# Edge logits and their per-node maxima: the leaky slope outside the loop, two of ten chunks raised on VectorE

## What is computed

```python
xj = h[src]                                   # h = x @ Wn.T + bn
a = leaky_relu(sum((xj + ee) * attn, -1), 0.01)   # one logit per edge
m = segment_max(a, dst)                       # greatest logit of each destination node
a = exp(a - m[dst])                           # the next phase takes it from here
```

## Time and profile before

| | us |
|---|---|
| median of 3 runs (lowest, highest) | 4043.22 (4040.58, 4044.01) |
| the profiled execution | 4043.18 |
| its span, first to last instruction | 4041.4 |
| loop of `phase_logits`, first ACT instruction to the last L1281's end | 2016.9 to 2446.9 |
| from there to the start of L1299's copy and its end | 2469.3 and 2472.7 |

### The profile page before, as it was taken

The page is one execution under the profiler, slowest core; times in us unless marked ns, Lnnn a source line. Parts: engine busy times, 40 slices in busy tenths (PEclk is TensorE's granted clock), DMA queues, the critical chain, the costliest instruction groups (busy, mean ns, idle before and its releaser), DMA issues. The chain is left out here.

```text
span 4041.4 us, 85100 instructions
## 1 busy us (share of the span) xinstructions
PE 3184.0 (79%) x17887; PEld 2358.5 (58%) x17888; DVE 2484.0 (61%) x6663; ACT 1822.0 (45%) x6302; POOL 1312.2 (32%) x1050
## 2 busy tenths in 40 slices
PE   5666667899887767999843335889999899999978
PEld 4444446888776655767632224778888444444455
DVE  7999998888775553244488886777666400001754
ACT  1888882344455532011298874777776000000111
POOL 1788888888888700101000000000000100003922
PEclk9999999999998878999855557999999999999989
DMA  2444443667888854757565553544332543541057
GB/s 95 126 122 124 120 118 86 197 203 241 242 248 277 279 219 132 212 169 210 163 213 185 180 165 107 157 125 121 111 97 78 186 140 117 190 154 42 0 191 262
DMA packets 430402, 646.79 MB, mean 160 GB/s; under 512 B 102666, under 2 KB 286737, under 8 KB 430176
## 3 DMA queue, kind: packets, MB, share of 16 engines
q1 hardware_dynamic: 344348, 511.68, 41.0%
q10 hardware_dynamic: 54388, 122.22, 8.4%
q0 software_dynamic: 31568, 11.67, 3.3%
HBM read 436.88 MB, written 207.57 MB: 159 GB/s over the span
## 5 line engine op out<-in xcount | busy, mean ns | idle before, releaser
L1065 POOL DMA_INDIRECT slots<-all_B,put_index x800 | 1050.4, 1313 | 343.1 <-issue 338.9
L2340 PE MATMUL gio_po<-gio_T,all_A 125*128 125x500 f32 (+1 forms) x1400 | 531.0, 540 | 7.7 <-DMA gio_T<-pair 7.7
L2340 PEld LDWEIGHTS gio_po<-gio_T,all_A 125*128 125x128 f32 x1400 | 249.8, 190 | 285.7 <-issue 276.4
L1315 ACT ACTIVATE lm_raised<-lm_hot,srt_words 128x125 f32<-128x125 bf16 x1200 | 356.3, 385 | 83.7 <-DVE lm_top L1230 66.8
L1349 PE MATMUL lm_ps<-lm_v,lm_node 125*128 x1220 | 170.5, 184 | 267.2 <-DVEq L1217 95.0
L1036 PE MATMUL put_ps<-put_right_in,put_left_in 128*128 128x125 f32 x2210 | 320.1, 295 | 66.5 <-ACT put_left_in L893 65.8
L2073 PE MATMUL att_ps<-att_right,att_left 128*125 128x125 f32 x2380 | 313.6, 284 | 71.4 <-ACT att_right L2094 57.9
L2073 PEld LDWEIGHTS att_ps<-att_right,att_left 128*125 128x125 f32 x2380 | 283.4, 190 | 97.6 <-issue 86.8
L1036 PEld LDWEIGHTS put_ps<-put_right_in,put_left_in 128*128 128x128 f32 x2210 | 282.0, 202 | 90.8 <-ACT put_left_in L893 76.6
L2147 DVE SCALAR_TENSOR_TENSOR att_power<-soft_negated,srt_words,att_far 128x125 f32 (+1 forms) x1190 | 321.1, 345 | 3.8 <-ACT att_right L2094 3.3
L1651 PE MATMUL c_po<-c_halves,c_T 125*125 125x512 f32 x1250 | 320.1, 405 | 0.0
(11 more groups left out here) (454 smaller groups left out, 5596.5 us busy)
## 6 DMA issues: line engine op xcount, KB each, us to landing
c_T<-counts SPq DMA_DIRECT2D x255, 312.5 KB, 3.3
pair<-put_T ACTq DMA_DIRECT2D x125, 625.0 KB
att_ring<-hot SPq DMA_DIRECT2D x480, 160.0 KB
gio_T<-pair SPq DMA_DIRECT2D x60, 1250.0 KB, 5.8
hot<-put_hot SPq DMA_DIRECT2D x448, 160.0 KB
all_A<-in_edge_attr_dram SPq DMA_DIRECT2D x100, 448.0 KB
lm_planes<-src_rows SPq DMA_DIRECT2D x123, 320.0 KB, 3.6
counts<-put_T ACTq DMA_DIRECT2D x125, 312.5 KB
```

The lines of the kernel that those rows point to most:

```text
L1065: nc.gpsimd.indirect_dma_start(slots, bass.IndirectOffsetOnAxis(index[:, C * g + j:C * g + j + 1], 0), stage[:, C * g + j, :], None).then_ ...
L1315: ins = nc.scalar.activation(raised[:, j % 2, c * P:(c + 1) * P], hot[:, j, c * S:c * S + P], ACT.Copy, scale=logit[:, ds(G * g + c, 1)])
L2340: ins = t_.matmul(po[:, i % 2, h, 0:w], A[:, b, 128 * h:128 * h + 128], tiles, start=(b == 0), stop=(b == NB - 1))
```

## The change

The loop's two slope instructions go: `total` now ends with one instruction that subtracts `floor` from the sum, adds the edge's own term and writes the logit. `logit` then holds unsloped values over the floor (of unsloped sums). After the loop `slope` adds the floor back and applies the slope to the whole `logit` in place, and the same to the maxima of 125 x 25.

ACT raises eight chunks of ten (LIFTS = 8). DVE takes the running maximum of those with 128x1000 elements, and for the last two chunks multiplies one-hot by logit and takes the maximum in one instruction each, straight from `hot`. As DVE now reads `hot`, SP waits, before it loads into a ring slot, on `grouped` as well as on `lifted`; the head of `grouped` is 3 instead of 2, so that SP's `wait_ge(grouped, g + 1)` asks for DVE's `greater` of group g-3.

```diff
                         sp.wait_ge(lifted, g + 1)
+                        sp.wait_ge(grouped, g + 1)
                         sp.sem_inc(passed, 1)
...
-                    chain(v.tensor_tensor(z[:, :], z[:, :], logit[:, ds(G * g, G)], ALU.add))
-
-                def logits(chain, g):
                     at = logit[:, ds(G * g, G)]
-                    chain(v.scalar_tensor_tensor(z[:, :], z[:, :], 0.01, z[:, :], ALU.mult, ALU.max))
-                    v.tensor_scalar(at, z[:, :], floor[:, :], None, ALU.subtract).then_inc(ready, 1)
+                    v.scalar_tensor_tensor(at, z[:, :], floor[:, :], at, ALU.subtract, ALU.add).then_inc(ready, 1)
+
+                def slope(t, parts):
+                    chain(v.tensor_scalar(t, t, floor[0:parts, :], None, ALU.add))
+                    chain(v.scalar_tensor_tensor(t, t, 0.01, t, ALU.mult, ALU.max))
...
-                    dve.wait_ge(grouped, g + 2)
+                    dve.wait_ge(grouped, g + 3)
+                    w = LIFTS * P
                     if first:
-                        ins = v.tensor_copy(top8[:, :], lift)
+                        v.tensor_copy(top8[:, 0:w], lift[:, 0:w])
                     else:
-                        ins = v.tensor_tensor(top8[:, :], top8[:, :], lift, ALU.max)
+                        v.tensor_tensor(top8[:, 0:w], top8[:, 0:w], lift[:, 0:w], ALU.max)
+                    for c in range(LIFTS, G):
+                        chunk, top = hot[:, ds(g % RING, 1), c * S:c * S + P].rearrange("p a n -> p (a n)"), top8[:, c * P:(c + 1) * P]
+                        if first:
+                            ins = v.tensor_scalar(top, chunk, logit[:, ds(G * g + c, 1)], None, ALU.mult)
+                        else:
+                            ins = v.scalar_tensor_tensor(top, chunk, logit[:, ds(G * g + c, 1)], top, ALU.mult, ALU.max)
                     ins.then_inc(grouped, 1)
...
+                turns = turns_of(dve, k)
+                dve.wait_ge(lifted, turns * RING + 3)
+                chain = Chain(dve, sloped)
+                slope(logit, L)
                 dve.wait_ge(turned, 1)
                 v.tensor_reduce(greatest[:, :], ps[0:P, 0:NB * L].rearrange("p (b l) -> p b l", l=L), AX.X, ALU.max).then_inc(ended, 1)
                 dve.wait_ge(ended, 1)
+                slope(greatest[:, :], P)
...
-                        act.wait_ge(grouped, g + 1)
-                        for c in range(G):
+                        act.wait_ge(grouped, g + 2)
+                        for c in range(LIFTS):
```

More of the change, by code:

```diff
@@ L1144, in phase_logits @@
         bounded, gathered, floored, cleared = (s.sem(n) for n in ("bounded", "gathered", "floored", "cleared"))
-        split, chain_sem = s.sem("split"), s.sem("chain")
+        split, chain_sem, sloped = s.sem("split"), s.sem("chain"), s.sem("sloped")
         expanded, looked, summed, ready, lifted, grouped = (
@@ L1148, in phase_logits @@
         joined, passed, turned, ended = (s.sem(n) for n in ("joined", "passed", "turned", "ended"))
-        PZ = 4
+        PZ, LIFTS = 4, G - 2
         with nc.Block() as block:
@@ L1246, in _ @@
                 chain(v.tensor_reduce(low[:, 0:2], bank(7)[0:1, 0:2 * L].rearrange("p (t l) -> p t l", t=2), AX.X, ALU.min))
-                chain(v.tensor_tensor(low[:, 2:3], low[:, 0:1], low[:, 1:2], ALU.add))
-                v.scalar_tensor_tensor(low[:, 3:4], low[:, 2:3], 0.01, low[:, 2:3], ALU.mult, ALU.max).then_inc(bounded, 1)
+                v.tensor_tensor(low[:, 2:3], low[:, 0:1], low[:, 1:2], ALU.add).then_inc(bounded, 1)
                 dve.wait_ge(gathered, 2)
                 chain(v.tensor_copy(floor[:, :], bank(7)[:, 256:257]))
-                for sem, head in ((summed, PZ), (grouped, 2), (joined, 1), (expanded, 2)):
+                for sem, head in ((summed, PZ), (grouped, 3), (joined, 1), (expanded, 2)):
                     dve.sem_inc(sem, head)
@@ L1256, in _ @@
                 expand(2)
-                logits(chain, 0)
                 dve.wait_ge(ready, 1)
                 total(chain, 1)
-                logits(chain, 1)
                 n = chain.n
@@ L1264, in step @@
                 def step(g, first):
-                    chain = Chain(dve, chain_sem, n + 3 * g)
+                    chain = Chain(dve, chain_sem, n + g)
                     expand(g + 3)
@@ L1268, in step @@
                     total(chain, g + 2)
-                    logits(chain, g + 2)
                     greater(g, first)
-                    assert chain.n == 3
+                    assert chain.n == 1
                 with dve.Fori(0, NB) as d:
@@ L1279, in _ @@
                         step(g, False)
-                    dve.wait_ge(grouped, g1 + 2)
+                    dve.wait_ge(grouped, g1 + 3)
                     v.tensor_reduce(tops[:, ds(d, 1), :].rearrange("p a n -> p (a n)"),
@@ L1335, in _ @@
                 pe.wait_ge(bounded, 2)
-                t_.matmul(bank(7)[:, 256:257], ones[0:1, :], low[:, 3:4], start=True, stop=True).then_inc(gathered, 1)
+                t_.matmul(bank(7)[:, 256:257], ones[0:1, :], low[:, 2:3], start=True, stop=True).then_inc(gathered, 1)
                 pe.wait_ge(split, 1)
```

## The result

| | before | after |
|---|---|---|
| median of 9 runs each (lowest, highest), us | 4043.15 (4040.22, 4046.09) | 4051.22 (4047.16, 4057.93) |
| the profiled execution's span | 4041.4 | 4049.2 |
| loop: start of the copy to `floor` to the last block reduction's end | 441.2 | 440.8 |
| tail: from there to the start of the copy of the spread maxima | 22.5 | 27.1 |
| next phase (`att_...`): from the clearing of `all_total` to the start of DVE's last `all_B<-att_ps` copy | 643.0 | 649.6 |

A forecast was written before the change was run, and what follows sets the result against it. DVE was taken to set the loop's time at 2.94 us a step. To 4043.18 us came -1 ahead of the loop, +5 in it and +5.5 behind it, +9.5 in all: 4052.7 us, range 4040 to 4066.

The forecast's parts named there:

- DVE's step by itself: DVE's loop step without the added wait falls from 2.94 to 2.79 us, in 94 steps 14 us.
- The first step: A block's first loop step gains nothing: the 2.95 us to the next L1216 is PE's look-up time and stays.
- The wait: SP's added wait for the end of DVE's step: 3.04 us a step where it lasts, loop 3.6 us slower.
- the recurrence: Loop rule: a step starts at least 3.2 us (mean) after the end of the step two before; loop 3.6 us slower.
- Rival 3: SP's path is a tenth longer or a chunk instruction costs 0.30: loop +15 instead of +5, 4063 us; chance 0.15.
- The last steps: Loop steps at a block's end, where DVE reduces and SP catches up: 0.15 us less each, 3.6 us.
- Landings: In the loop, the one-hots' and planes' landings that hold SP now lie on the path: +1.4 us.
- the 1 ahead of it: Ahead of the loop, two slope pairs go: 1 us less.
- The tail: After the loop, the slope over all logits, partly covered by DVE's 5.70 us wait for PE, and over the maxima: +5.5 us.
- Rival 2: After the loop, writing every second word is slow: slope passes up to 18.6 us, tail +15, 4062 us; chance 0.13.
- The next phase: The attended phase behind the tail, with unchanged code: the sum had no term for it.

The follow-up runs named there:

- without SP's wait: The changed kernel without SP's added wait, DVE's two chunk instructions reading chunks that ACT raised instead of the one-hots: 4036.28 us, ratio 0.9986 to before.
- SP reordered: The changed kernel, all waits kept, with SP issuing the planes' part two indices ahead of the one-hots' part: 4036.57 us, ratio 0.9983 to before.
- The wait alone: The kernel before with only SP's added wait on DVE's maximum (`grouped`, head 3): 4052.80 us, ratio 1.0025.
- the kernel with 56 more instructions: The changed kernel with 56 unneeded semaphore increments in DVE's idle time ahead of the wait on `turned`: 4041.84 us, ratio 0.9995 to before.

## Why the prediction came out as it did

- **DVE's step by itself**: right. 2.84 in after and 2.83 without SP's wait, against 2.79, and 1.64 from the maximum to L1211 as was forecast; a chunk pair with the step back to L1211 takes 0.52 to 0.60, where 2 x 0.26 was summed.
- **The first step**: right for after. "It gains nothing" holds up to the next L1216: 2076.61 to 2079.64 in after is 3.03 us, and the step's own 0.18 us more is given back by a wait for PE that is gone. It hides only so much: with the slope in the loop as well, the same two chunks cost 0.55, and the stretch is 3.32 us.
- **The wait**: right in place and in kind, as waits of 18.2 us for SP and the reordering show. In the first and middle steps after lost 0.18 x 25 + 0.03 x 69 = 6.7 us against before; the recurrence, taken without the last steps, had about 7. Rival 3, the same recurrence with a longer path, is refuted by that. But the agreement is partly luck: DVE's own gain in these steps was 7 us (before against SP reordered), where 69 at 0.15 are 10, and the wait cost 14, where the recurrence had 17 to 18. The wait alone shows the same: 8.9 us where it gave 14.
- **The last steps**: mis-sized. They were summed at 0.15 less each, 3.6 us. They are 0.26 less, 6.3 us, because the idle time between the block reduction and the next expansion fell as well, to 0.61 us from 0.77.
- **Landings**, +1.4: on the path, and of that size, at one place. In SP's waits the one-hots' landing makes up 2.6 us in four waits.

```profile
SPq L1193 <- DMA lm_hot<-hot: 2.6, 4, 1.4
```

The longest, 1.4 us, ends at 2123.97, and DVE's expansion at 2125.12 then waits 1.39 us for SP, with no back edge in between. It is among the 6.7 us above. With all this the loop is -0.4 instead of +4 (the 5, less the 1 ahead of it): 2.7 of the difference are the last steps, and 1.9 the recurrence and the landings together.
- **The tail**: right, +4.7 against +5.5. It begins 1.17 us after the reduction (1.3 summed), the passes take 2.82 and 5.36 (2.8 and 5.4), the wait of L1301 for PE is gone, the small pair is 0.24 and 0.19. Writing every second word has no price here: 5.36 us for 4992 elements are 1.07 ns each, and 0.57 in the first pass. Rival 2 is refuted. The Trainium skill (Vector Engine (DVE) Microarchitecture Reference, Measured stream behaviour on trn2) gives 1.71 ns per column for a destination that hops 4 KiB every element, and says that a port streams at the full rate only while its elements come in runs of at least two adjacent words. For a step of two words, of which its table has no row, the trace disagrees with that rule, and the measurement decides.
- **The next phase**: the step that failed. The sum had nothing behind the tail and gave no reason for it; no code there changes. 6.6 us came from it, and they stand where the loop's overestimate stood, so that the total agreed within 1.5 us. Without them, by the kernel with 56 more instructions, the change can't be told from before (0.9995, 0.9986 to 1.0004; its phase is 1.9 us shorter than before's, which flatters it by that much). That the change is slower by 0.2% thus hangs on a side effect, and the range held the time partly by luck.

## What to carry to other kernels

Take a change apart before summing it up: here one half (an elementwise step moved out of a loop that DVE bounds, onto an array at the end) is worth 28 us and the other half more than costs that, and split off, with its second pass put under a wait that was there anyway, the first half makes the kernel 0.8% faster. When an engine takes over a read from a ring, the new wait on the loader's queue costs by what is queued behind it, not by itself; put the loads for the next stage ahead of it. And where a phase with unchanged code changes its time, compare the pitches of the same instructions in the two traces before looking for a reason in the data.

## What the runs showed of the hardware

- **The place of the code in an engine's queue has a price.** Eight more instructions on DVE ahead of a loop made one of its three copies of the body slower: a row of ten by 0.09 us, the pitch between the groups by 0.2, and a phase of 643 us longer by 6 to 7. With 64 more it was gone, and the first block, slow in before too (2.78 us a ten), ran at 2.69 as well, so that the phase was shorter than before's. Single pitches in the slow rows show one of the ten at over 0.3 us where the others have 0.26, in one kernel always the same one of a copy of the body; in the first block it is the fourth in before and the second with eight more instructions, in the later blocks of after the eighth. The step from the branch at the loop's end to the next instruction is 0.28 to 0.30 us in the slow blocks and 0.17 to 0.20 in the fast ones. What the queue does at these places, and why the first pass over a slow copy can be fast, no run shows.
- A tensor of two-word step is as fast as a contiguous one for reading and for writing in place on DVE: 2.82 us for 4992 elements with one tensor operand (contiguous, 0.68 us for 1000), 5.36 with two (1.07 ns each; contiguous, 250 elements more or less of the maximum are 0.26 us, 1.04 ns each).
- A chunk of 128x125 with a factor per partition, scaled and compared in one instruction, is 344 ns long at a pitch of 0.26 us, and the pitch is what it costs. L1305, a 125x125 instruction with such a factor and one tensor operand, comes at a pitch of 0.20 (25 in 4.95 us). What sets the two pitches was not taken apart.
